# Attention weights turned by f32 products with the identity in place of TensorE transposes

## What is computed

```python
xn = _layernorm(input1)
xh = xn.reshape(B, T, H, d)                      # B 32, T 128, H 8, d 16
Q = einsum('bthd,hd->bht', xh, Wq)
K = einsum('bthd,hd->bht', xh, Wk)
V = einsum('bthd,hde->bhte', xh, Wv)
A = -(Q[:, :, :, None] - K[:, :, None, :]) ** 2
P = softmax(A / d ** 0.5, axis=-1)
O = einsum('bhts,bhse->bhte', P, V)
return O.transpose(0, 2, 1, 3).reshape(B, T, E) @ Wm + input1
```

## Time and profile before

| | |
|---|---|
| median of 3 runs | 813.37 us (813.32 to 814.0) |
| the profiled execution | 808.0 us, its span 806.1 us |
| PE busy | 457.3 us, 57% of the span, 2558 matmuls |
| PE weight loads | 391.2 us, 2559 |
| DVE busy | 529.5 us, 66% |
| ACT busy | 377.1 us, 47% |
| POOL busy | 228.4 us, 28% |
| transposes of line 616 | 256, 113.2 us, 449 ns each |
| products of line 621 | 512 matmuls, 111.7 us, 301 ns each |

### The profile page before, as it was taken

One profiled execution on the slowest core, in us unless ns is written; L12 is line 12 of the kernel. 1 busy time (PEld: TensorE's weight loads), 2 busy tenths in 40 slices (PEclk: granted clock), 3 DMA queues, 4 the chain that ended last, 5 costly groups with the idle time before them and its releaser, 6 DMA issues.

```text
span 806.1 us, 12967 instructions
## 1 busy us (share of the span) xinstructions
PE 457.3 (57%) x2558; PEld 391.2 (49%) x2559; DVE 529.5 (66%) x1931; ACT 377.1 (47%) x1099; POOL 228.4 (28%) x417
## 2 busy tenths in 40 slices
PE   1300000000002689999799998212999999999960
PEld 0200000000001567787678887211888888888850
DVE  2789999999747876988986756460444444444425
ACT  1344444454302877777566663101444544454520
POOL 1054545455300000000412431553223332333330
PEclk9999999999999755555555555555999999999985
DMA  4499430403254131235000000112111111111119
GB/s 90 79 171 166 85 68 18 85 1 85 45 141 131 53 91 53 66 92 148 27 11 18 28 24 11 36 48 60 34 45 42 46 42 45 41 42 45 46 31 286
DMA packets 113000, 53.92 MB, mean 67 GB/s; under 512 B 56780, under 2 KB 108748, under 8 KB 112867
## 3 DMA queue, kind: packets, MB, share of 16 engines
q1 hardware_dynamic: 106366, 44.60, 24.0%
q0 software_dynamic: 4352, 8.47, 3.2%
q10 hardware_dynamic: 2237, 0.38, 0.3%
HBM read 29.68 MB, written 24.26 MB: 67 GB/s over the span
## 4 chain that ended last, share of the span: by engine, by line
PE 46%; DVE 29%; issue 7%; DMA 6%; ACT 6%; SPq 3%; POOL 3%; ACTq 0%; POOLq 0%; DVEq 0%
PE ps L722 9%; PE ps L616 8%; PE ps L621 6%; PE ps L532 5%; DVE D L1106 4%; PE ps L533 4%; DVE D L1115 4%; PE ps L534 4%; PE ps L712 4%; POOL xd_dram L1003 3%; DVE ps L1095 3%; PE ps L596 3%; ACT ps L789 3%; ACT D L795 3%; DMA xd_dram<-pay,slot 1%
## 5 line engine op out<-in xcount | busy, mean ns | idle before, releaser
L1003 POOL DMA_INDIRECT xd_dram<-pay,slot x64 | 64.3, 1004 | 260.7 <-DVE pay L1353 243.3
L621 PEld LDWEIGHTS ps<-va,pt 128*128 128x128 f32 x512 | 133.6, 342 | 0.0
L616 PE MATMUL ps<-eye_sb,sq 128*128 128x128 f32 x256 | 113.2, 449 | 12.9 <-DVE on L1295 10.9
L1029 POOL DMA_INDIRECT y_dram<-on,dest x72 | 70.7, 982 | 158.0 <-DVE on L1424 120.6
L621 PE MATMUL ps<-va,pt 128*128 128x17 f32 x512 | 111.7, 301 | 0.0
L1402 DVE TENSOR_TENSOR sq<-sq,ps 128x512 f32<-128x512 f32 x72 | 49.5, 688 | 90.6 <-PE ps L534 67.5
L568 PE MATMUL ps<-zdiag,ones_f 32*128 32x32 f32 x2 | 0.6, 406 | 182.4 <-DVE zdiag L1183 182.4
L616 PEld LDWEIGHTS ps<-eye_sb,sq 128*128 128x128 f32 x256 | 86.3, 338 | 33.1 <-issue 27.1
L987 POOL TENSOR_TENSOR D<-D 128x128 f32<-128x128 f32 x130 | 56.2, 433 | 120.6 <-DVE D L1129 60.9
L568 PEld LDWEIGHTS ps<-zdiag,ones_f 32*128 32x128 f32 x2 | 0.5, 306 | 182.5 <-DVE zdiag L1183 182.5
L935 ACT ACTIVATE sq<-ps 128x512 f32<-128x512 f32 x72 | 43.2, 600 | 83.2 <-PE ps L534 83.2
(11 more groups left out here) (203 smaller groups left out, 1145.6 us busy)
## 6 DMA issues: line engine op xcount, KB each, us to landing
stage<-xd_dram SPq DMA_DIRECT2D x72, 65.0 KB
D<-th_dram SPq DMA_DIRECT2D x16, 208.0 KB, 4.7
g_dram<-D SPq DMA_DIRECT2D x14, 208.0 KB, 4.6
x_dram<-D SPq DMA_DIRECT2D x14, 208.0 KB, 4.7
h0q<-g_dram SPq DMA_DIRECT2D x8, 256.0 KB, 2.9
gb<-g_dram SPq DMA_DIRECT2D x8, 256.0 KB, 3.3
xf<-x_dram SPq DMA_DIRECT2D x8, 256.0 KB, 3.1
xb<-x_dram SPq DMA_DIRECT2D x8, 256.0 KB, 3.8
```

What stands on the lines that cost most here:

```text
L616: last = nc.tensor.transpose(ps[:, 5 + h // 4, T * (h % 4):T * (h % 4) + T], sq[n % 3][:, T * h:T * h + T], eye_sb[:])
L621: m = nc.tensor.matmul(ps[:, 7, (HD + 1) * h:(HD + 1) * (h + 1)], pt[turned % 2][:, T * h:T * h + T], va[q % 2][:, k, h, :], start=True, s ...
L1003: pool.indirect_dma_start(xd_dram, bass.IndirectOffsetOnAxis(slot[:, q, j, k:k + 1], 0), pay[q % 2][:, k, j, :], None).then_inc(s_sc[2 * k ...
L1029: pool.indirect_dma_start(y_dram, bass.IndirectOffsetOnAxis(dest[:, c:c + 1], 0), yrow[c], None, bounds_check=2 * NB * T - 1, oob_is_err=F ...
```

## The change

Line 616 calls a plain matmul with the same two operands and the same place for the result, in place of a transpose. The batch's P is still the stationary operand and the identity `eye_sb` the moving one. Waits, semaphores, order and buffers are the same. The other transposes of the kernel stay.

```diff
                 for h in range(NH):
                     if n < NB:
-                        last = nc.tensor.transpose(ps[:, 5 + h // 4, T * (h % 4):T * (h % 4) + T],
-                                                   sq[n % 3][:, T * h:T * h + T], eye_sb[:])
+                        last = nc.tensor.matmul(ps[:, 5 + h // 4, T * (h % 4):T * (h % 4) + T],
+                                                sq[n % 3][:, T * h:T * h + T], eye_sb[:], start=True, stop=True)
                         if h == NH - 1:
                             last.then_inc(s_ptp, 1)
```

## The result

| | before | changed |
|---|---|---|
| median of 4 runs | 813.35 us (813.21 to 814.0) | 875.52 us (870.09 to 879.63) |
| the profiled execution | 808.0 us, span 806.1 | 870.1 us, span 868.3 |

The ratio is 1.076, with a 95% interval of 1.068 to 1.084: the change costs 62 us. The forecast was 880 us, with a range from 848 to 892.

What follows compares the result with a forecast made beforehand. The prediction took lines 616 and 621 on the tensor engine at 1.2 GHz to bound the attention. Heads 78.8, absorbed waits -8.8, lost rise +2.0, new rises -5 gave +67 us: 813.4 to 880 us, range 848 to 892.

Steps and rivals of the forecast that it cites:

- What bounds: Lines 616 and 621 on the tensor engine set the end for nearly all the attention, with the clock at its lower level.
- The price of a head: A turn of P with its product of line 621: 0.854 us after the change, 0.318 us more than 0.536.
- Both terms: Per head in lines 616 and 621: an added record of 0.214 us, and about 0.1 us of saving lost with the short load.
- The lower bound: In the pair, the second load hides and only the added record of 0.214 us counts: 854 us, chance 8%.
- What is absorbed: Tensor engine waits that go as DVE catches up, before line 659, line 596 and for normalise: 8.8 us (bounds none or 18).
- The three waits for `normalise` that were to go: Tensor engine waits of 1.53, 1.20 and 0.3 us, part of the 10.9 us for normalise, expected to vanish.
- What was to stay: The rest of the 10.9 us wait for normalise, as DVE's chain starts when the tensor engine ends a step.
- The clock: In the attention: one or two rises take 5 us off; the loss of the earlier rise at 381.6 us adds 2.0.
- The sum: Whole kernel: 78.8 - 8.8 + 2.0 - 5 = +67 us, profiled 875 us, median 880 us.
- The reading of the 269 us rise: The clock's first recorded rise followed twelve back-to-back transposes, some 3 us, without f32 products; taken as evidence against the skill's rule.
- The first rival: Products hold 2.4 GHz in turn_and_attend, a head takes 0.445 us, DVE becomes the bound: about -25 us, 788 us, chance 8%.
- The signs: Line 616: 512 matmuls, 0.33 us loads; heads 0.85 us apart; DVE about 20 us of 40; line 659's wait gone; POOL near 567.

Runs made afterwards that it cites:

- e1: The kernel before with each turn of P made twice, as a transpose, into the same place: 843.7 us, where the kernel before took 806.4.
- e2: The kernel before with a step's eight transposes issued first and the products of line 621 behind them: 815.4 us against 806.4.
- e8: The changed kernel with normalise ahead of second_norms and first_norms in DVE's order: ratio 1.064 (1.062 to 1.066) to the kernel before.
- e9: The kernel before with a step's turns first, each made twice as a transpose, and the products of line 621 behind them: 804.9 us against 806.6.
- e7: The changed kernel (turns as products) with 112 columns moved by line 621 in place of 17: 813.0 us, ratio 0.999 to the kernel before.
- e4: The kernel before with normalise ahead of second_norms and first_norms in DVE's order: 805.5 against 806.4 us, ratio 0.999.
- e10: The kernel before with 96 columns moved by line 621 and normalise ahead of second_norms and first_norms in DVE's order: 791.5 us against 806.6, ratio 0.982.
- e6: The kernel before (turns as transposes) with 64 columns moved by line 621 in place of 17: 804.9 us, ratio 0.989.
- e5: The kernel before (turns as transposes) with 96 columns moved by line 621 in place of 17: 804.5 us, ratio 0.991.
- e3: The changed kernel with a step's eight turns, now products, issued first and the products of line 621 behind them: 820.3 us against 806.4, ratio 1.017.

## Why the prediction was right

**What bounds.** As read: the pair on the tensor engine, at 1.2 GHz. Steps of the pipeline grew by 2.56 us where the clock was low (in step 22 the eight heads took 4.29 us before, 430.90 to 435.19, and 6.85 after, 474.28 to 481.13).

**The price of a head.** Forecast 0.854 us, measured 0.855. Both terms have been separated: 0.213 us for a second record (e1: 0.749 less 0.536) and 0.106 us for records of a product with their long loads (0.855 less 0.749). The 0.230 us of a transpose's load came from line 651; inside the pair the loads of line 616 last 370 ns in median in the kernel before, longer than those of a product, so how long a load lasts there doesn't show what it costs, and the saving rests on the starts and on e1 and e2. The lower bound, that the second load hides, was wrong: that rival is out. 31 x 2.56 = 79.4 us, forecast 78.8.

**What is absorbed.** Forecast 8.8 us. I compared the 31 steps one by one in the two timelines, the time between the last head of a step and the first of the next: where the kernel before had a wait that the changed one has not, it shrank by 9.5 us in all. The largest is the wait at 390 us, 4.3 us, of which 0.7 is left. The three waits for `normalise` that were to go (1.53, 1.20 and 0.3 us) went. Yet the total for `normalise` fell by only 0.7 us, since three others grew, at 416, 456 and 541 us, from 0.94, 0.87 and 0.14 us to 1.50, 1.13 and 1.58; the first two stand in a rise of the clock. What was to stay did: the waits of 1.62, 0.87 and 3.52 us before heads, every fourth step, are in both timelines within 0.01 us in the first half of the attention. Two of them in the changed kernel (1.63 and 0.88 before):

```profile
337.94 0.77 PE L616 MATMUL ps<-eye_sb,sq 128*128 128x128 f32 x2 [1.62 <-DVE on L1295]
...
376.30 0.77 PE L616 MATMUL ps<-eye_sb,sq 128*128 128x128 f32 x2 [0.87 <-DVE on L1295]
```

And their cause was the one named, DVE's order behind the end of a step: e8 took most of them away by order (though other waits came in their place), e2 by an earlier end of the turns.

**The clock.** This was the term off in size. Forecast: one or two rises, 5 us, less the 2.0 us that the kernel before had from its own, so 3 us net. Measured: four rises, of 20.5 us. The eight heads of the 31 steps grew by 71.0 us in place of 79.4, 8.4 us less, and other work in the rises gave about 1 more: 9.4 us net, 6 more than forecast. Dense work at a rise was as expected: `turn_inputs` and `merge` stand before all four (before 413.8 us PE was busy for 3.40 of 3.40 us), as they did before the rise at 381.6 us in the kernel before. What I had not reckoned with is that the higher level may hold for a second stretch when the pairs fill it without waits (492.3 to 495.6 us, 3.30 of 3.30 us busy).

**The sum.** 79.4 - 9.5 - 9.4 = 60.5 us in the attention, 1.3 us behind it, 0.4 ahead: 62.2, the difference of the spans. Forecast 67. The 5 us are the clock's. Most of the 1.3 us is too: step 32, which has no turns, ran at 2.4 GHz before (1.71 us) and at 1.2 GHz after (3.27), a gift of the kernel before that the forecast did not count. The forecast of the median, 880 us, added 5.4 us to the profiled run's; the measured median lies 5.4 us above it as well, and that is luck, since it is the middle between two pairs of runs, 870 to 871 and 880 us.

**The clock, weighed.** The rule of the Trainium skill ("TensorE: Matmul & The Clock Gate", Part 4) that the higher clock does not engage for transposes does not hold in this kernel: sixteen grouped transposes in a step brought 78 us of 160 at 2.4 GHz (e9). The reading of the 269 us rise was right. The first rival's price of a head was right, 0.44 us where the clock is up. Its time was not reached: e7, at 2.4 GHz for 125 of 160 us, took 813 and not 788 us. The change then costs nothing, but it gains nothing either. The rival counted DVE's busy share and too little of the engine's waits for DVE, 33 us in e7; how much of the 25 us this is was not run.

**The signs.** Named rightly: 512 records, 0.33 us loads, 0.85 us heads, the wait at line 659, the unchanged 306 us behind. Wrong: DVE "20 us in place of 27" in a stretch of 40 us. From 420 to 460 us DVE was busy for 27.7 us, from 460 to 500 for 24.1: with longer steps the same stretch holds earlier batches, and before 420 us DVE had more to do (34.4 us of 40 in the earlier trace rows); that this is the whole reason was not worked out. The wait of 4.3 us before line 659 is not quite gone, 0.7 us is left. POOL's last sends started at 560.6, not at 567, which is the same miss as the sum.

## What to carry to other kernels

Count an f32 turn by its records and loads, in the order in which they are issued: a transpose is one record with a short load, a product with the identity two with long ones, and beside load-bound products the long loads add half as much again as the record. Before pricing anything on the tensor engine, read its granted clock: here the level was worth as much as the whole change (e7), and more moved columns in records that wait for their load anyway raised it, at no cost up to 64 columns. When a reorder takes a wait away, add up all waits before giving it the credit: in e4, e8 and e10 the wait for `normalise` fell by 6 to 26 us and the idle time as a whole by 2 us at most, and what was gained in e8 and e10 was mostly clock. It is still worth trying again after each change of the bound (nothing in e4, 1% in e8 and e10).

## What the runs showed of the hardware

- Moving 64 or 96 columns in place of 17 in records that take 0.21 us for their load raised the time at 2.4 GHz from 3 to 51 and 81 us of 160 (e6, e5), and made the kernel 1% faster; with `normalise` ahead, 1.5 to 1.8%.
- With sixteen transposes grouped in a step (e9) the clock was at 2.4 GHz for 78 us of 160; the same sixteen between the products of line 621 (e1) gave 6 us.
- At 1.2 GHz a head, a turn and its two records of line 621, took 0.536 us with one transpose, 0.749 with two, and 0.855 with the two records of a product.
- The same instructions in another order (e3 against the changed kernel) had 59 in place of 6 us of 160 at 2.4 GHz.
- The kernel before took 806 us on two chips and 814 on a third; the ratio of the changed kernel was 1.076 beside a kernel before of 813 us and of 806.6 us.
